# Context product in one block, row biases first, 192 channels laid as 128 and 64, and VectorE's next moments and mask ahead of the denominator in the tail

## What is computed

```python
# 1: a small vision transformer, 2 layers, 128 channels, 8 heads of 64
x = patches @ conv_w + conv_b                    # 2048 -> 128
for i in range(2):
    y = ln(x); q, k, v = split(y @ qkv_w[i])     # 3 x 512
    q = softmax(q, over the 64 of a head) * 64 ** -0.5
    k = softmax(k, over the 256 tokens)
    ctx = k.T @ v                                # 64 x 64 for each head
    x = x + (q @ ctx) @ out_w[i] + out_b[i]
    y = ln(x); x = x + gelu(y @ ff1_w[i] + ff1_b[i]) @ ff2_w[i] + ff2_b[i]
h = ln(x) @ head_w + head_b                      # 128 -> 192
# 2: linear attention, 192 channels, 12 heads of 16, phi(z) = elu(z) + 1
q, k, v = split(ln(h) @ W_qkv); q, k = phi(q), phi(k)
kv = k.T @ v; z = 1 / (q . (sum of k over the tokens + phi(0)) + eps)
h = h + (q @ kv * z) @ W_out + b_out
# 3: MLP 192 -> 768 -> 192; its weights are scaled in blocks of 48 by mixed coefficients
h = h + gelu_tanh(ln(h) @ W0.T + b0) @ W1.T + b1
```

## Time and profile before

| | |
|---|---|
| device time, median of 3 runs | 126.88 us (125.83 to 127.46) |
| device time of the profiled execution | 125.87 us |
| its span | 124.1 us |
| PE / PEld busy | 115.3 / 104.7 us |
| DVE / ACT / POOL busy | 80.7 / 65.3 / 52.6 us |
| granted TensorE clock, mean | 1.0 |
| loads, most of them before 30 us | 11.5 MB |

### The profile page before, as it was taken

The page is one execution under the profiler, slowest core; times in us unless marked ns, Lnnn a source line. Parts: engine busy times, 40 slices in busy tenths (PEclk is TensorE's granted clock), DMA queues, the critical chain, the costliest instruction groups (busy, mean ns, idle before and its releaser), DMA issues.

```text
span 124.1 us, 2489 instructions
## 1 busy us (share of the span) xinstructions
PE 115.3 (93%) x934; PEld 104.7 (84%) x934; DVE 80.7 (65%) x241; ACT 65.3 (53%) x148; POOL 52.6 (42%) x62
## 2 busy tenths in 40 slices
PE   6999899999999999999999999499959999999992
PEld 6999799997788889898898888399846989999991
DVE  1000467988999868998599965767887897345002
ACT  4000445925369984999799946354504182521520
POOL 0000262079648742597427965469853230050000
DMA  4999999986700000000000000000000000000101
GB/s 106 359 411 411 402 419 400 416 310 174 177 2 0 0 5 3 0 0 5 0 0 0 0 5 3 3 0 0 5 0 0 0 0 0 5 0 25 39 0 63
DMA packets 3947, 11.63 MB, mean 94 GB/s; under 512 B 448, under 2 KB 1568, under 8 KB 3936
## 3 DMA queue, kind: packets, MB, share of 16 engines
q1 hardware_dynamic: 3936, 11.48, 25.5%
HBM read 11.09 MB, written 0.39 MB: 92 GB/s over the span
## 4 chain that ended last, share of the span: by engine, by line
PE 40%; ACT 17%; DMA 13%; DVE 12%; SPq 6%; POOL 6%; issue 4%; DVEq 0%; POOLq 0%
DMA rows_sb<-in_rows 13%; PE bank L340 9%; PE bank L479 6%; PE bank L574 6%; ACT kexp L1101 5%; PE bank L346 4%; ACT L1129 3%; PE bank L431 3%; ACT q L1107 3%; PE bank L438 2%; PE bank L557 2%; SPq L293 2%; DVE xn L741 2%; DVE stats L726 2%; ACT yT_hi L1073 2%
## 5 line engine op out<-in xcount | busy, mean ns | idle before, releaser
L1228 POOL TENSOR_TENSOR rstd<-mv,minus_half 128x2 f32<-128x2 f32 x14 | 10.4, 740 | 36.7 <-DVE mv L730 36.7
L1101 ACT ACTIVATE kexp<-bank,nkmax 128x256 f32<-128x256 f32 x16 | 7.4, 474 | 6.4 <-DVE nkmax L801 6.4
L1242 POOL TENSOR_TENSOR xb<-x,rows_sb 128x256 f32<-128x256 f32 x8 | 5.8, 730 | 9.4 <-DMA rows_sb<-in_rows 6.1
L1096 ACT ACTIVATE qkvw_hi<-qkvw 128x512 fp32r<-128x512 f32 x6 | 3.5, 622 | 11.7 <-DMA qkvw<-in_qkv_w 11.7
L363 PE MATMUL bank<-embed_sb,patches_sb 128*128 128x128 f32 x64 | 8.5, 280 | 0.6 <-DMA patches_sb<-in_patches 0.6
L363 PEld LDWEIGHTS bank<-embed_sb 128*128 128x128 f32 x64 | 8.8, 219 | 0.2
L363 PE MATMUL bank<-embed_sb 128*128 128x128 f32 x64 | 8.9, 305 | 0.0
L1247 POOL TENSOR_TENSOR qn<-q,rqsum 128x512 f32<-128x512 f32 x8 | 8.3, 1042 | 1.3 <-DVE rqsum L824 1.3
L479 PE MATMUL bank<-restw,hid 128*128 128x128 f32 x64 | 8.1, 280 | 0.6 <-ACT hid L1129 0.6
L448 PE MATMUL bank<-cw,qT 128*128 128x128 f32 x64 | 8.6, 278 | 0.0
L363 PEld LDWEIGHTS bank<-embed_sb,patches_sb 128*128 128x128 f32 x64 | 7.8, 191 | 1.0 <-DMA patches_sb<-in_patches 0.8
(11 more groups left out here) (135 smaller groups left out, 325.2 us busy)
## 6 DMA issues: line engine op xcount, KB each, us to landing
patches_sb<-in_patches SPq DMA_DIRECT2D x4, 512.0 KB, 10.3
embed_sb<-in_embed SPq DMA_DIRECT2D x2, 768.0 KB, 6.6
restw<-in_rest_w SPq DMA_DIRECT2D x2, 768.0 KB, 15.2
embed_sb<-in_embed SPq DMA_DIRECT2D x2, 384.0 KB, 7.9
qkvw<-in_qkv_w SPq DMA_DIRECT2D x3, 256.0 KB, 9.0
qkvw<-in_qkv_w SPq DMA_DIRECT2D x1, 768.0 KB, 15.5
embed_sb<-in_embed SPq DMA_DIRECT2D x1, 576.0 KB, 4.0
projw_raw<-in_proj_w SPq DMA_DIRECT2D x1, 576.0 KB, 16.5
```

The lines of the kernel that those rows point to most:

```text
L1101: nc.scalar.activation(kexp[i][:, c, :], KB[c // 2][:, (c % 2) * TOKENS:(c % 2 + 1) * TOKENS], ACT.Exp, bias=nkmax[i][:, c:c + 1], accum_o ...
L1228: nc.gpsimd.tensor_tensor(rstd[i][:], mv[i][:, :, 1], minus_half[:], ALU.pow).then_inc(rstd_ready[i], 1)
```

## The change

It has four parts.

1. **Context product in one block.** PE's order becomes `turn_q` of tile 0, one `context_out` with all eight matmuls, `turn_q` of tile 1. Inside, neighbours differ in rows and columns of the array: (a, b) = (0,0), (1,1), (0,1), (1,0). ACT copies tile 0 of q first, then scales pairs 0, 2, 3, then copies tile 1; the scalings on ACT and DVE wait for the whole block.
2. **Row biases first.** The load of `rows_sb` is issued ahead of `restw[0]`, `qkvw[1]` and `mix_sb`.
3. **192 channels as 128 and 64.** The first chunk has channels 0 to 127, the second channels 128 to 191 twice, in both halves of the partitions. The second chunk's activations (`yT3_end`) keep the high part in the upper half and get the low part in the lower; the second chunk of the low weights is zero in the lower half. So two matmuls give all three parts of the 64 channels: with the high weights (high + low activations) and with the low weights. A product has five matmuls and not six: two under "high", three under "low". `norm_apply` gets one more instruction for each token tile, which writes the 64 channels a second time (L755), and `turn_norm3` and POOL's `after_norm` wait for all four. Two memsets are added at the start of DVE's list. The loads of `aqkv_w` and `fc_w` grow by a third.
4. **The tail on DVE.** For image 0 the other image's moments go ahead of `q3_times_k_sum`, and in both images `kv3_masked` goes ahead of `k3_denominator`.

```diff
             second(3)
+            sp.dma_start(rows_sb[:], rows.to_broadcast([P, NROW])).then_inc(loaded["rows"], 16)
             sp.dma_start(restw[0][:], rest_w[0]).then_inc(loaded["rest0"], 16)
             sp.dma_start(qkvw[1][:], qkv_w[1]).then_inc(loaded["qkv1"], 16)
             sp.dma_start(mix_sb[:], mix).then_inc(loaded["mix"], 16)
-            sp.dma_start(rows_sb[:], rows.to_broadcast([P, NROW])).then_inc(loaded["rows"], 16)
...
-            def context_out(l, i, a):
-                if a == 0:
-                    pe.wait_ge(loaded[f"rest{l}"], 16)
-                    pe.wait_ge(ctxs_ready[i], l + 1)
+            def context_out(l, i):
+                pe.wait_ge(loaded[f"rest{l}"], 16)
+                pe.wait_ge(ctxs_ready[i], l + 1)
                 for c in range(0, PAIRS, 2):
-                    for b in range(2):
+                    for a, b in ((0, 0), (1, 1), (0, 1), (1, 0)):
...
+            def parts3(i, which):
+                if which == "high":
+                    return [(yT3_hi[i], 0, 0), (yT3_hi[i], 1, 0)]
+                return [(yT3_lo[i], 0, 0), (yT3_end[i], 0, 1), (yT3_end[i], 1, 1)]
+
+            def product3(dst, i, which, tokens, weights, at, weight_is_left):
+                order = parts3(i, which)
+                for k, (y, part, c) in enumerate(order):
+                    pair = (y[:, tokens], weights[part][:, c, at])
+                    left, right = pair[::-1] if weight_is_left else pair
+                    mm = nc.tensor.matmul(dst, left, right, start=(which == "high" and k == 0),
+                                          stop=(which == "low" and k == len(order) - 1))
+                return mm
...
-                context_out(l, i, 0)
                 turn_q(l, i, 0)
                 if s == 0:
                     pe.wait_ge(x_ready[1], TILES)
-                context_out(l, i, 1)
+                context_out(l, i)
                 turn_q(l, i, 1)
...
+                    if width == E:
+                        nc.vector.tensor_scalar(xn[i][:, t, E:EP], src[:, t, P:E], mv[i][:, t, 0:1],
+                                                rstd[i][:, t:t + 1], ALU.subtract, ALU.mult).then_inc(xn_ready[i], 1)
...
+                if c == 0:
+                    nc.vector.tensor_tensor(yT3_lo[i][:], bankof[:, 0:TOKENS], yT3_hi[i][:].bitcast(F32), ALU.subtract)
+                else:
+                    end = yT3_end[i][REST:P, :]
+                    nc.vector.tensor_tensor(end, bankof[REST:P, 0:TOKENS], end.bitcast(F32),
+                                            ALU.subtract).then_inc(yT_lo_ready[i], 1)
...
+            for w in (aqkvw_parts[1], fcw_parts[1]):
+                nc.vector.memset(w[REST:P, 1, :].bitcast(F32), 0.0).then_inc(end_zeroed, 1)
...
             h_from_head(1)
+            norm_stats(1, LN3, h[1], E, h_ready[1], 1, 0)
             q3_times_k_sum(0)
-            norm_stats(1, LN3, h[1], E, h_ready[1], 1, 0)
+            kv3_masked(0)
             k3_denominator(0)
-            kv3_masked(0)
...
-                context_scaled(l, i, 0)
-                context_scaled(l, i, 2)
                 q_to_sbuf(l, i, 0)
-                context_scaled(l, i, 3)
+                for c in (0, 2, 3):
+                    context_scaled(l, i, c)
                 q_to_sbuf(l, i, 1)
```

132 lines of the change are left out of this document (63 added, 69 removed).

## The result

The changed kernel takes 122.98 us (median of 4 runs, 122.81 to 123.62) against 126.9 us before (4 runs, 125.83 to 127.46): a ratio of 0.971, with a 95% interval from 0.964 to 0.978. It is faster. The forecast was 124.3 us with a range from 122.6 to 125.8. The profiled execution took 122.81 us with a span of 121.0, against 125.87 and 124.1 before: 3.1 us less, where the sum of the prediction gives 2.5.

What follows compares the result with a forecast made beforehand. PE was taken as busy 115.3 of 124.1 us, bounding from image 1's turned q on, with DVE waits before. Terms -0.1 -0.5 -0.5 -0.3 +0.4 -0.3 -1.2 = -2.5 gave 124.3 us beside the 126.88 median, range 122.6 to 125.8.

Steps and rivals of the forecast that it cites:

- steps 1 and 2: Context block in one group: eight matmuls in about 5 slots, 0.6 us saved on PE, -0.5 us arriving in each step.
- step 3: Context block there: -0.3 us, since ACT's second copy of q, ending at 46.25 in step-1 times, holds the second attention.
- step 0: Early row biases: POOL's `rstd` starts up to 0.37 us sooner beside DVE's `weighted`; -0.1 us arrives.
- at the same rate of loss: Step 0: `rstd` loses 0.53 us per 0.67 of overlap with `weighted`, so it ends at 30.6.
- norm 1: Two added 64-wide instructions at 0.2 us each delay `xn` and PE behind it: +0.4 us.
- `fc3`: PE-bound end of the tail: ten remaining products each save one 0.12 us matmul, -1.2 us.
- norms 2 and 3 with part 4: Tail on DVE: moments fill a 0.54 us wait, norms cost 0.4 each; `turn_q3(1)` at 103.95, not 104.25: -0.3 us.
- DVE's chain from there to `qn` is as long as before: Behind norm 3: from the sum of k, starting at 100.5 and not 100.82, DVE's way to `qn` keeps its length.
- Row tiles do not overlap: Rival for the context block: gains only 0.2, 0.2 and 0.1 us in the steps, 125.2 us; chance 0.16.
- dear norms: Rival: extra norm instructions cost 0.3 us each; norms 2 and 3 with part 4 +0.1, norm 4 +0.1; 125.1 us; chance 0.10.
- `rstd` not slowed: Rival for step 0: `weighted` does not slow `rstd`, 0.3 us more gained, 124.0 us; chance 0.10.
- `restw[0]`: Slower rival in step 0: load landing after 26.4 delays ACT, DVE and PE; at 28, 128.5 us; chance 0.04.

Runs made afterwards that it cites:

- e5: Changed kernel with the context block's quarter order (0,0), (0,1), (1,0), (1,1), neighbours sharing rows; 124.01 us in one run.
- e1: Changed kernel with its part 1 undone, the context product in two groups with q's transposes between; 125.49 us, median of 10, ratio 0.989 to the kernel before.
- e2: Changed kernel with its part 2 undone, row biases loaded behind the mixing masks again; 123.89 us, median of 4, ratio 0.978 to the kernel before.
- e9: Changed kernel with DVE's `weighted` moved behind image 1's normalisation in step 0, away from `rstd`; profiled time 123.71 us.
- e3b: Kernel before with parts 1, 2 and 4 but 96 and 96 channels, the same kernel as e3, run once more for a profile; 125.13 us.
- e12: Changed kernel without the two 64-wide instructions per 192-wide norm; second chunk transposed 64 wide, low part written to rows 64 to 127; 121.61 us in one run.
- e3: Kernel before with parts 1, 2 and 4 of the change, channels left as 96 and 96; 124.47 us, median of 4, ratio 0.979 to the kernel before.
- e13: As e12, but each transpose waits only for its own tile's normalisation; 123.1 us, 6 runs, ratio 0.973 to the kernel before.
- e14: The kernel of e12 run six times; 122.33 us, ratio 0.9675 to the kernel before.

## Why the forecast came out as it did

**Right: steps 1 and 2** (-0.50, -0.48 for -0.5) and their place. But the model behind them was too careful. It let two matmuls run at once and the next pair start half a pass later, about 5 slots for eight matmuls. Four run at once, 4 slots for sixteen (e5), and the second eight cost nothing. Against it stood that no row showed matmuls on different rows; the pair of the earlier trace rows, which shares even its rows and doesn't wait, already spoke for it. The Trainium skill, "TensorEngine Tiling (Array Packing)", section Tiling Modes, has tiles that load and multiply in parallel and a drain when the mode changes. The trace agrees with both: x4 at 43.30, and 0.17 us of PEld idle at each change. That the sum was right all the same is luck, for two errors cancel: from the block to the second transposes 0.60 us pass for the 0.69 forecast (43.89 to 44.58), but from there to the attention 0.65 for 0.52. ACT has q until 44.01 and starts its three pieces at 44.04, 0.88 us for all; that PE waited for the first is likely, but the trace names no releaser there.

**Mis-sized: step 3** (-0.65 for -0.3). The step that failed is "the copy at 46.25 ... holds it". Timelines of PE and ACT before, then of the same after:

```profile
75.01 2.16 PE L448 MATMUL bank<-cw,qT 128*128 128x128 f32 x16
```

```profile
75.36 0.59 ACT L1123 ACTIVATE qT<-bank 128x512 f32<-128x512 f32 x1
```

```profile
72.88 2.07 PE L457 MATMUL bank<-cw,qT 128*128 128x128 f32 x16
```

```profile
73.13 0.60 ACT L1141 ACTIVATE qT<-bank 128x512 f32<-128x512 f32 x1
```

The copy stands 0.25 us behind the first attention's start now, 0.35 before, because the last piece no longer waits for a second group. It was before that the copy held the second attention: PE's first eight weight loads were over at 75.87, the ninth came at 76.05, behind the copy's end at 75.95; now the ninth comes at 73.82 directly behind the eighth, and the copy has ended at 73.73. The second `add_attention` followed the first one after 1.03 us (1.03 in e1 too), now after 0.87. So the change took a hold of 0.16 away where the forecast put one of 0.2 in.

**Mis-sized: step 0** (-0.59 for -0.1), the largest miss. The failed step is "at the same rate of loss". `rstd` is not slowed by `weighted` but shut out until it ends, and `weighted` itself had been shut out by POOL's `qn`, which the early biases moved out of its way (e2, e9). The forecast had both facts in view, `qn` 1.5 us earlier and 1.17 for `weighted`, and didn't join them. It also took image 1's moments for what bounds the stage; before, POOL's wait for the biases did. Part of the miss is chance: 0.17 of the 0.59 came from the earlier start. The Trainium skill, "SBUF — State Buffer", section Who interferes with whom, says that an instruction of VectorE with two SBUF inputs and one of GpSimd that reads SBUF exclude each other, and whoever is first has the ports to its end. The trace agrees: 0.63 us from the end of `qn` to that of `weighted`, 0.56 from there to that of `rstd`. The forecast read off that rule a gain of 0; it looked at one of the two locks only.

**Right: norm 1** (+0.35 for +0.4) **and `fc3`** (1.21 by e3b, ten times 0.12). In norm 1 two errors cancel in part. The instructions cost 0.45, and the stretch without them is 0.10 shorter than in the kernel before (e12, 12.11 us for 12.22 from step 3's last `add_attention`); that should be the matmuls saved behind the norm, which the forecast put at nothing, and no run shows it by itself. PE's wait there, 0.4 among the signs, is 0.33: its last matmul ahead of the transposes starts at 80.13 and they start at 80.58, where 0.12 lie between in e12. The 64-wide instruction takes 0.31 us by itself and 0.22 from start to start, for 0.2 taken.

**Mis-sized: norms 2 and 3 with part 4** (+0.06 for -0.3). Part 4 gives 0.27 and not 0.53: the wait of 0.54 was counted as gained whole, when what fills it is longer than the wait, and left a gap where it had stood. Norm 3 costs 0.46 (e12): its `xn` starts 0.67 earlier against `h_from_head(1)` as forecast (0.7), but ends 0.23 and not 0.35 earlier. And "DVE's chain from there to `qn` is as long as before" failed: from PE's sum of k to `qT` 1.24 us pass (98.73 to 99.97) for 0.95. The late transposes hold the low part of v, and DVE's copy of v behind it starts 0.08 after the sum of k, where it was 0.05 ahead (0.13), and the two low parts take 0.17 longer, 0.43 each from start to start for 0.36. The terms are then -0.27, +0.46, +0.17 and a rest of -0.30 for +0.06; the rest should be the saved matmuls of `qk3(1)` and `v3(1)`, and no run shows it by itself. Norm 2 was nearly free (0.03).

**Rivals.** "Row tiles do not overlap" is refuted by e1 and e5; "dear norms" is refuted in its price (0.22 us for an instruction and not 0.3) and for norm 4, though its sum for norms 2 and 3, +0.1, is nearer to the measured +0.06 than the forecast's -0.3; "`rstd` not slowed" named the right place but not the cause; `restw[0]` landed by 23.0, not 26.4 (and by that rival's own rule, one for one beyond 26.4, a landing at 28 with the other terms of the forecast gives 125.9 us and not the 128.5 it names); the row biases moved 0.59 us and not nothing. Of the signs, `rstd` in step 0 took 1.14 us and not more than 1.2.

The sum gives 126.88 - 2.5 = 124.4, written as 124.3. The 1.4 us between 124.4 and 122.98 are thus 0.6 of the sum and 0.8 of the level: the forecast was laid beside the median 126.88, which stood 1.0 above its profile, the changed kernel's 0.2. The level is chance, since it hangs on how many of three or four runs are at full clock. And the 0.6 of the sum are a balance of misses: 0.5 and 0.35 too little in step 0 and step 3, 0.36 too much in norms 2 and 3.

## What to carry to other kernels

When two engines' instructions last longer beside each other than alone, write down which ended first and by how much the other outlasted it; if the remainder stays the same where the overlap differs, as here (0.63 us for overlaps of 0.54 and 0.82), they exclude each other, and moving an instruction on one engine can free one on the other and, through it, the next one on its own. A wait that is filled with work from elsewhere gives the wait less what the work overruns it, less what the work had been filling where it stood. Small matmuls of four quarters belong in one block, here in either of two orders, and the width of a partition split is worth choosing so that the engine that bounds the stage gets fewer instructions, as long as the layout is made by a write to other rows and not by further instructions of the engine that is next.

## What the runs showed of the hardware

- Four 64-row, 64-column matmuls start within 0.04 us of each other, sixteen are over after 0.67 us, in either order of quarters (changed kernel, e5).
- DVE's two-input product and POOL's reading instructions exclude each other in both directions: 0.75 became 1.17 and 1.45 us, 0.70 became 1.14, 1.23 and 1.25 (changed kernel, before, e2; alone in e9).
- DVE may write rows 64 to 127 from inputs in rows 0 to 63 at the usual price: 0.42 us for 64 x 256 (e12), 0.43 in the changed kernel with all in the same rows.
- TensorE's clock fell for a stretch in 19 of 36 runs of the kernel before and in 15 of 44 of the changed kernel and the experiments. In the profiles of e3, e3b, e5, e13 and e14 it fell at 78 to 80 us, in e1 at 95, where PE had been busy no more than elsewhere. In e5 PE was busy for all of the 2 us from 72, for 1.54 of those from 74 and 1.47 of those from 76, and from 79 to 82 us the granted clock was 0.51. In e1 PE was busy for 2.87 of the 4 us from 76, 3.22, 3.48 and 3.42 in the next three windows, and then came these (window; length, busy time and count by engine; granted clock, DMA share, GB/s):

```profile
92.00:96.00 4.00, 2.89 (x15) 2.34 (x16) 3.32 (x11) 1.46 (x3) 1.02 (x2) 0.88 0.00 0
96.00:100.00 4.00, 4.00 (x19) 4.00 (x18) 2.33 (x7) 0.00 (x0) 0.51 (x1) 0.69 0.00 0
```

  These means of 0.88 and 0.69 are full speed (2.4 GHz) and half of it (1.2 GHz) mixed; from 96 to 98 us it is 0.50. Against the changed kernel e1 lost 1.6 us there (2.25 late at image 1's `xn`, 3.60 at `h2` of image 0, 3.86 at image 1's q times sum of k). Why it falls in one execution and not in another of the same kernel stays open: e12 and e14 are the same program, one at full clock throughout and one not.
